# Graph attention, two layers: adjacency in 1 MB transfers onto 128 partitions, and node rows read back by column block

## The reference

```
h = max(layernorm(x), 0)
x = x + L0(h, adj);   h = max(layernorm(x), 0);   x = x + L1(h, adj)

L(h, adj):                       # W, b, a1, a2 of the layer
    H = h @ W + b                # 8192 x 128
    e[i, j] = leaky(H[i] . a1 + H[j] . a2)        # slope 0.2
    e[i, j] = -9e15 where adj[i, j] == 0
    return softmax(e, over j) @ H
```

## Time and profile before

| | |
|---|---|
| median of the runs | 2206.73 us |
| profiled execution: its own time | 2236.48 us |
| profiled execution: span | 2234.6 us |
| mean granted PE clock | 0.974 |
| PE busy | 2001.2 us, 90% |
| DVE busy | 1773.5 us, 79% |
| ACT busy | 1139.9 us, 51% |
| moved by transfers | 357.46 MB |

### The profile page before, as it was taken

How to read it: one execution, slowest core, us unless ns; L and a number is a source line. 1 busy time by engine, 2 the same in 40 slices (tenths; PEclk the granted TensorE clock), 3 DMA queues, 4 the chain that set the end, 5 groups by cost and what they waited for, 6 DMA issues and landing times.

```text
span 2234.6 us, 49031 instructions
## 1 busy us (share of the span) xinstructions
PE 2001.2 (90%) x16866; PEld 1698.2 (76%) x16866; DVE 1773.5 (79%) x2733; ACT 1139.9 (51%) x1097; POOL 318.6 (14%) x496
## 2 busy tenths in 40 slices
PE   5456889999988888899888879999999999999998
PEld 3234678887777777788777768888888888888887
DVE  6565778997777777789877678888888888888884
ACT  4455667886667677777777332222333333222331
POOL 6440112322111112222112300000000000000000
PEclk9997999999999999999999989999999999999999
DMA  5659999999999999999999650000000000000000
GB/s 140 167 138 231 258 273 297 339 277 271 269 265 256 259 269 275 283 303 286 279 271 277 176 108 29 28 28 28 28 27 27 28 28 28 28 28 28 28 28 9
DMA packets 117077, 357.46 MB, mean 160 GB/s; under 512 B 24624, under 2 KB 74032, under 8 KB 80176
## 3 DMA queue, kind: packets, MB, share of 16 engines
q1 hardware_dynamic: 114736, 340.23, 57.5%
q10 hardware_dynamic: 2304, 16.78, 1.9%
HBM read 314.84 MB, written 42.07 MB: 160 GB/s over the span
## 4 chain that ended last, share of the span: by engine, by line
PE 46%; DMA 37%; ACT 6%; SPq 4%; issue 3%; DVE 3%; DVEq 0%; POOL 0%; ACTq 0%; POOLq 0%
PE acc L541 45%; DMA adj_sb<-in_adj_dram 34%; ACT sign_a L603 5%; SPq L254 3%; DMA node_rows<-row_parts 2%; DMA mask_bytes<-pair_a 1%; DVE ext L793 0%; DVE masks L865 0%; ACT row_parts L591 0%; DMA masks<-in_x_dram 0%; PE ps_h L493 0%; SPq L280 0%; DVE row_parts L800 0%; DVE stats L713 0%; DVE centred L726 0%
## 5 line engine op out<-in xcount | busy, mean ns | idle before, releaser
L541 PE MATMUL acc<-node_rows,masks 128*128 128x258 f16 x16384 | 1888.4, 276 | 71.8 <-DVE masks L872 69.5
L541 PEld LDWEIGHTS acc<-node_rows,masks 128*128 128x128 fp8e4 x16384 | 1615.5, 99 | 325.6 <-issue 79.4
L603 ACT ACTIVATE sign_a<-adj_sb 128x2048 int8<-128x2048 int32 x256 | 489.1, 1910 | 285.0 <-DMA adj_sb<-in_adj_dram 284.2
L616 ACT ACTIVATE sign_z<-t_row,neg_s 128x2048 int8<-128x2048 f32 x256 | 504.4, 1996 | 2.0 <-DVE masks L865 1.9
L622 ACT ACTIVATE part_a<-acc,coef_a 128x258 f32<-128x258 f32 x128 | 60.2, 471 | 677.6 <-PE acc L541 677.6
L812 DVE TENSOR_SCALAR sign_z<-t_row,neg_s 128x2048 int8<-128x2048 f32 x256 | 326.9, 1278 | 2.9 <-issue 2.4
L872 DVE TENSOR_SCALAR masks<-masks 128x2048 uint32<-128x2048 uint32 x256 | 311.6, 1217 | 0.3
L865 DVE STREAM_TRANSPOSE masks<-sign_z 128x2048 uint32<-128x2048 uint32 x128 | 294.9, 2304 | 0.1
L892 DVE SCALAR_TENSOR_TENSOR part_ac<-acc,coef_c,part_a 128x258 f32<-128x258 f32 x128 | 61.9, 484 | 238.3 <-ACT part_a L622 238.3
L438 POOL TENSOR_TENSOR h_sum<-h_sum,ext 128x128 f32<-128x128 f32 x126 | 113.2, 898 | 736.9 <-DVE ext L793 733.3
L493 PE MATMUL ps_h<-w_ext,centred_t 128*128 128x133 f32 x256 | 80.9, 409 | 119.1 <-ACT centred_t L578 115.6
(11 more groups left out here) (83 smaller groups left out, 612.9 us busy)
## 6 DMA issues: line engine op xcount, KB each, us to landing
adj_sb<-in_adj_dram SPq DMA_DIRECT2D x1024, 256.0 KB, 11.1
node_rows<-row_parts SPq DMA_DIRECT2D x128, 129.0 KB, 9.2
node_rows<-node_rows SPq DMA_DIRECT2D x32, 516.0 KB, 12.3
mask_bytes<-pair_a ACTq DMA_DIRECT2D x16, 1024.0 KB, 10.8
pair_a<-mask_bytes SPq DMA_DIRECT2D x16, 1024.0 KB, 4.8
x_old<-in_x_dram SPq DMA_DIRECT2D x64, 64.0 KB, 12.6
x_after_layer<-x_new SPq DMA_DIRECT2D x64, 64.0 KB, 13.1
x_old<-x_after_layer SPq DMA_DIRECT2D x64, 64.0 KB, 1.8
```

The costliest lines, as they stand in the source:

```text
L541: mm = pe.matmul(acc[T.p][s][:, 0:ROW], stationary[s][:, c // BYTES, c % BYTES, :], node_rows[:, c, ROW * s:ROW * (s + 1)], start=(c == 0) ...
L603: nc.scalar.activation(sign_a[:, T.p, SPAN * r:SPAN * (r + 1)], adj_sb[:, r, :], ACT.Sign, scale=-1.0) \
L616: nc.scalar.activation(sign_z[:, T.p, SPAN * r:SPAN * (r + 1)], t_row[:], ACT.Sign, scale=-1.0, bias=neg_s[:, ds(RGROUPS * T.t + r, 1)]).t ...
```

## The change

A slot of adjacency is filled by one transfer of 1 MB onto all 128 partitions; its source is written with the column block outermost, then the 32 rows. Its semaphore is then raised by 16 where it was raised by 64, and ACT waits for that. The second layer's node rows are read back by `reload_block`, one transfer for each column block b: its four node tiles 16a + b go onto 128 partitions, again with the quarter a outermost in the source. A block waits only for its own tiles: the last four blocks are issued as the row stores of tiles 60 to 63 land. The first layer's rows are read as before.

```diff
-                for a in QUAD_ORDER:
-                    sp.nop(nofuse=True)
-                    sp.dma_start(adj_sb[QROWS * a:QROWS * (a + 1), r, :],
-                                 adj[ds(T.t * TILE + QROWS * r, QROWS), SPAN * a:SPAN * (a + 1)]) \
-                      .then_inc(adj_loaded[r], 16)
+                sp.nop(nofuse=True)
+                sp.dma_start(adj_sb[:, r, :],
+                             adj[ds(T.t * TILE + QROWS * r, QROWS), :].rearrange("i (a c) -> a i c", a=QUADS)) \
+                  .then_inc(adj_loaded[r], 16)
...
+            def reload_block(b):
+
+                sp.dma_start(node_rows[:, BYTES * b:BYTES * (b + 1), :].rearrange("p k r -> p (k r)"),
+                             rows_dram[1].rearrange("(a b) (j k) r -> b a j (k r)", a=QUADS, k=BYTES)[b]) \
+                  .then_inc(S[1].rows_loaded[b // PER_GROUP], 16)
+
             def reload_rows(g):
-                for a in range(QUADS):
-                    if (a, g) != (QUADS - 1, VGROUPS - 1):
-                        load_rows(1, a, g)
+                for b in range(PER_GROUP * g, PER_GROUP * (g + 1)):
+                    reload_block(b)
...
             sp.wait_ge(S[0].tile_summed, TILES)
-            reload_rows(VGROUPS - 1)
+            store_rows(1, Tile(TILES - 2))
+            for k in range(TILES - 4, TILES - 2):
+                sp.wait_ge(S[1].rows_stored[k % 2], 16 * (k // 2 + 1))
+                reload_block(k % BLOCKS)
             store_x_new(0, Tile(TILES - 1))
-            store_rows(1, Tile(TILES - 2))
             store_rows(1, Tile(TILES - 1))
-
-
-            for p in range(2):
-                sp.wait_ge(S[1].rows_stored[p], 16 * TILES // 2)
-            load_rows(1, QUADS - 1, VGROUPS - 1)
+            for k in range(TILES - 2, TILES):
+                sp.wait_ge(S[1].rows_stored[k % 2], 16 * (k // 2 + 1))
+                reload_block(k % BLOCKS)
...
-                act.wait_ge(adj_loaded[r], 16 * QUADS * (T.t + 1))
+                act.wait_ge(adj_loaded[r], 16 * (T.t + 1))
```

More of the change, by code:

```diff
@@ L65 @@
 NODE_STEP = 4
-QUAD_ORDER = (0, 2, 1, 3)
 class Tile:
```

## The result

The changed kernel takes 3844.43 us, the median of 4 runs (3840.84 to 3846.52), against 2214.66 us (2205.22 to 2226.64) for the kernel before: a ratio of 1.7352, with a 95% interval of 1.7247 to 1.7458. It is slower, as forecast with 0.85, but the time is 1386 us under the forecast of 5230 and 6 us under the low end of the range. It came out near rival A (3900 us), which had a chance of 0.25. The profiled execution took 3840.84 us with a span of 3839.1.

The account below looks back on a forecast made before the run. Bound taken: adjacency through the DMA queue in the first layer, PE in the second. Profiled 2236.5 + 2866 (stream) + 45 (node stage) + 115 (row reads) = 5262, less 30 for the median: 5230 us; range 3850 to 6300.

Parts of the forecast that it names:

- rival A: Adjacency transfers on 4 engines that do not hinder each other, at 25.0 GB/s each: 3900 us, chance 0.25.
- Part (a), how many engines: First layer's merged 1 MB adjacency transfer: source with 4 outermost, so 4 engines instead of 16.
- Part (a), the rate of an engine: First layer's adjacency stream: 17.2 GB/s an engine, 62.7 us a tile, +2866 us; bounds +1638 at 25.0, +4038 at 13.3.
- The small transfers behind four 1 MB loads: First layer's x transfers and row stores on SP's queue: wait some 60 us instead of 12 to 13, adding nothing.
- Part (b): Node stage: the first tile's four adjacency loads occupy engines longer, delaying row stores ACT waits for; +45 us, 0 to 64.
- Part (c): Second layer's row reads: 16 transfers of 516 KB on 4 engines at 13.3 GB/s each, +115 us; +39 at 25.0.
- Part (d): Order of SP's waits at the end: one row store moves ahead of the last reads, under 2 us.
- C: Adjacency transfer spread over all 16 engines, each on its own 8 partitions, at PE's pace: 2045 us, chance 0.12.
- D: Adjacency transfer spread over 16 engines, but its packets meet as in the kernel before: 2207 us, chance 0.03.
- The share near a quarter: Sign in the first layer's profile: DMA share of 0.25 to 0.32.
- The other signs: First layer: 55 to 105 GB/s, some 60 us to landing, PE under 30%; second layer: row-read wait about 100 us.
- Only for that: First layer of the kernel before: ACT waits for adjacency, and nothing else, 115.9 us in 480.

Follow-up runs that it names:

- run 1: Kernel before, plus ten groups of transfers from SP and two from POOL after its last store, timing transfer forms alone: 2476.01 us against 2228.09.
- 5 and 6: Kernel before, still 256 KB quarters, with the source's rows named 4 outermost, then 8 outermost: 3771.08 us (ratio 1.7194), then 2503.09 us (1.1412).
- run 7: Kernel before, plus transfer groups after its last store (led quarters, 8 or 4 outermost, partition pairs): pairs 1 or 32 apart 30 GB/s, 4 or 64 apart 49.
- run 2: Kernel before with only the adjacency part of the change, rows read back by quarter as before: 3800.13 us, ratio 1.7353.
- run 4: Changed kernel with the adjacency source written as 128 rows of one column block, words landing in another arrangement: 2139.88 us, ratio 0.9758 to the kernel before.

## Why the prediction was wrong in its size

**Part (a), how many engines: right.** Four, and because of the source's outermost number: runs 1, 5 and 6 show it by changing that number alone.

**Part (a), the rate of an engine: this step failed.** It said "At 17.2 GB/s that is 62.7 us a tile" and gave +2866 us; the stream took 41.0 us a tile and +1499.9. With 1.081 MB on each of the 4 engines that is 26.4 GB/s. The step's reason was that the four shares "start on transfers together and march in step". That is seen in the first microseconds of run 1, at 67 GB/s, and then it is over: 106. In stretches of 3 us from 2190 the rate of run 1 climbs 55, 68, 60, 82, 93 at a share of 0.23 to 0.27 all along, while packets of some 0.61 us give way to packets of 0.309 us. Partitions 0 and 32 do share a way in (30 GB/s for two, run 7), but four engines on 128 partitions need not be on partitions that share one, and from 600 to 800 us of the changed kernel they seldom are: its 8 KB packets took 311 ns in the mean. So the engines come apart within some 15 us and stay apart, as rival A had it; what drives them apart was not tried. The rate of before was no property of an engine, but of 16 engines on 32 partitions; I carried it over to a transfer with a quarter of the engines and four times the partitions. The row that fitted was the lone 128-partition load, and its 25.0, which I took as the upper bound, was itself too low, since its stretch held the start of the transfer (packets of up to 1.35 us, and 309 ns from then on); that is why even rival A's +1638 was over the +1499.9, and the time fell under the range. That A's total came within 60 us is in part luck: its stream was 138 us too long and its node stage 43 too short.

**The small transfers behind four 1 MB loads: right that they cost nothing on top.** The store of x landed after 33.4 us where it took 13.1 (some 60 was forecast, by the failed rate), and nothing came of it: 4.72 MB at the stage's 115 GB/s are 41.0 us, so the tiles follow one another as fast as the bytes arrive.

**Part (b): +45 forecast, +63.1 measured,** the top of the text's range of 0 to 64. The wait is the one that was named: up to the start of the stream ACT waited 109.7 us for row stores, in 7 waits, where it waited 46.0. Here the engines did hinder each other. The node stage's stretches above have 97 GB/s at a share of 0.51, 11.9 GB/s for a busy engine; at that rate a 1 MB load takes 4 engines 22 us, not the 15.2 of the text, and four of them 4 x (22 - 3.8) = 73. The packets agree: from 50 to 110 us the middle 8 KB packet took 629 ns. In the stream there is little beside adjacency; here rows are stored and read back at the same time. Which of these meet was not tried.

**Part (c): +115 forecast, 44 measured** by the difference to run 2: the +34.4, and 9.3 in the piece before it, which takes 63.4 us here and 54.1 in run 2. The rate failed in the same way (13.3, read where 16 engines crowd on 32 partitions), and again the time is near the 25.0 bound (+39). The two long waits are where the text had them, in the first tile of the second layer. A third, not in the text, stands before that tile: a row store issued behind the first four reads took 20.7 us to land, and ACT waited 10.29 us for it before it could scale the last rows; in the kernel before there is no such wait.

**Part (d)** is not to be seen apart from (c).

**Rivals.** C's condition, 16 engines, was not met by this kernel; where run 4 met it, PE became the bound as C says, but the time was 2139.88 us and not 2045. The 4-engine reads of rows are some 44 of these 95 us, and the rest is open. D falls with the share of 0.28.

**Signs and readings.** The share near a quarter was as written. The other signs missed with the rate: 115 GB/s and not 55 to 105, 38 us to landing and not 60, PE busy 48% and not under 30% (part of that is the clock: the same products took longer at 0.72), 31 us of waits for row reads and not 100. "Only for that", of ACT's waits for adjacency, was too strong: in the same stretch ACT waited another 28 us for DVE and PE, which changes nothing in the sum.

## What to carry to other kernels

Before a transfer is merged, write down what stands outermost on both of its sides: a source of [4][32][2048] gives a quarter of the core's DMA engines (3844 us) where [128][2048] gives all (2140 us), and the size and the partitions of the destination do not make up for it. A DMA share in the profile near 0.25 or 0.5 under a queue that is never empty is the sign of it. And a rate for one engine, read where 16 engines crowd on 32 partitions, says nothing of 4 engines on 128: look for the row whose destination is alike, or bound by the fastest row with room above it.

## What was not expected of the hardware

- A DMA share of 1.0 does not say that the engines are fast. 16 engines busy all the time moved 428 GB/s onto 128 partitions, 206 to 243 in quarters of 32, and 89 when POOL's four transfers wrote the same partitions. Eight engines at a share of 0.51 moved 214 (run 7, the group with 8 outermost), nearly what 16 move in quarters.
- Two engines on partitions 1 or 32 apart get 30 GB/s together, on partitions 4 or 64 apart 49. An 8 KB packet takes 309 ns when nothing meets it, and took 527 ns in the middle of the kernel before's first layer.
- SP's issue is held back by a full queue of few engines: 4.9 us for a 516 KB transfer on 4 engines, while an issue of the same size onto all 16 took 0.45 us when the queue was short.
- The kernel before is unsteady: 76 us between its fastest and slowest of 18 runs, against 3 us in 4 runs with 8 engines, whose packets meet nothing. That the meetings make it so is likely and not shown.
